# Attention with int8 feed-forward on one core: weights handed over transposed, split by scales from sums of squares or maxima, and values laid into key ranges through DRAM

## What is computed

```python
def _L0_attn_ref(x, wq, wk, wv, wo):
    ...
    q = (x @ wq.T).reshape(b, t, N_HEADS, HEAD_DIM).transpose(0, 2, 1, 3)
    k = (x @ wk.T).reshape(b, t, N_KV_HEADS, HEAD_DIM).transpose(0, 2, 1, 3)
    v = (x @ wv.T).reshape(b, t, N_KV_HEADS, HEAD_DIM).transpose(0, 2, 1, 3)
    ...
    scores = jnp.einsum('bhtd,bhsd->bhts', q, k_full) / np.sqrt(HEAD_DIM)
    mask = _sink_window_mask(t)[None, None, :, :]
    attn = _masked_softmax(scores.astype(jnp.float32), mask).astype(x.dtype)
    out = jnp.einsum('bhts,bhsd->bhtd', attn, v_full)
    out = out.transpose(0, 2, 1, 3).reshape(b, t, N_HEADS * HEAD_DIM)
    return out @ wo.T
...
x = x + _L0_attn_ref(_layernorm(x, axis=-1), L0_attn_wq, L0_attn_wk, L0_attn_wv, L0_attn_wo)
x = x + _L0_ffn_ref(_layernorm(x, axis=-1), L0_ffn_weight, L0_ffn_bias)
```

## Time and profile before

| what | value |
|---|---|
| median of 3 runs | 634.7 us (633.99 to 635.71) |
| profiled execution | 634.63 us, span 632.8 us |
| PE busy | 599.3 us (95%) |
| DVE busy | 544.8 us (86%) |
| ACT busy | 399.7 us (63%) |
| POOL busy | 307.8 us (49%) |
| mean granted clock of PE | 0.987 |

### The profile page before, as it was taken

How to read it: one execution, slowest core, us unless ns; L and a number is a source line. 1 busy time by engine, 2 the same in 40 slices (tenths; PEclk the granted TensorE clock), 3 DMA queues, 4 the chain that set the end, 5 groups by cost and what they waited for, 6 DMA issues and landing times.

```text
span 632.8 us, 18148 instructions
## 1 busy us (share of the span) xinstructions
PE 599.3 (95%) x7589; PEld 529.5 (84%) x7589; DVE 544.8 (86%) x1084; ACT 399.7 (63%) x631; POOL 307.8 (49%) x302
## 2 busy tenths in 40 slices
PE   5759999999999999999999999999999999999983
PEld 4547888889898988989898888989898888989872
DVE  5876899989898988989898998989898998988885
ACT  5676766566666666666666666667666666665740
POOL 1142445464565546455554646456554745535440
PEclk9989999999999999999999999999999999999996
DMA  9931401213040311203040221304030120304000
GB/s 295 352 103 20 116 1 49 55 35 85 3 117 2 86 34 46 73 15 105 1 120 2 67 52 37 83 9 112 3 96 24 53 68 20 99 1 118 3 18 34
DMA packets 33841, 41.31 MB, mean 65 GB/s; under 512 B 3936, under 2 KB 24416, under 8 KB 33760
## 3 DMA queue, kind: packets, MB, share of 16 engines
q1 hardware_dynamic: 33616, 40.02, 22.9%
q10 hardware_dynamic: 144, 0.13, 0.1%
HBM read 10.26 MB, written 4.19 MB: 23 GB/s over the span
## 4 chain that ended last, share of the span: by engine, by line
PE 87%; DVE 7%; ACT 3%; issue 1%; POOL 1%; DMA 1%; POOLq 0%; SPq 0%; ACTq 0%
PE ps L551 26%; PE ps L429 25%; PE ps L456 7%; PE ps L396 7%; PE ps L405 6%; PE ps L512 5%; PE ps L533 4%; PE ps L534 4%; PE ps L384 1%; PE ps L578 1%; DVE WoT L1008 1%; DVE Qs L892 1%; PE ps L566 1%; PE ps L336 1%; DMA X<-in_L_attn_x 1%
## 5 line engine op out<-in xcount | busy, mean ns | idle before, releaser
L429 PE MATMUL ps<-xT,WqT 128*128 128x256 f16 x1536 | 178.2, 273 | 2.0 <-DVE WqT L1008 1.3
L551 PE MATMUL ps<-WoT,pool 128*128 128x256 f16 x1536 | 178.0, 273 | 0.2 <-DVE pool L916 0.2
L429 PEld LDWEIGHTS ps<-xT,WqT 128*128 128x128 f16 x1536 | 147.0, 98 | 19.1 <-issue 3.0
L551 PEld LDWEIGHTS ps<-WoT,pool 128*128 128x128 f16 x1536 | 147.5, 98 | 16.4 <-DVE pool L916 0.3
L1203 POOL TENSOR_TENSOR small<-E,rr 128x576 f32<-128x576 f32 x63 | 72.6, 1152 | 99.8 <-DVE rr L911 99.8
L775 ACT ACTIVATE pool<-ps 128x512 f16<-128x512 f32 x128 | 69.5, 595 | 81.7 <-PE ps L534 81.6
L1209 POOL TENSOR_TENSOR PP<-small,PP 128x576 f16<-128x576 f32 x63 | 80.9, 1284 | 68.2 <-ACT PP L768 68.2
L735 ACT ACTIVATE Qs<-ps 128x576 f16<-128x576 f32 x128 | 82.4, 644 | 43.6 <-PE ps L429 43.6
L1195 POOL TENSOR_TENSOR Sm<-Sm,mx 128x576 f32<-128x576 f32 x64 | 73.7, 1152 | 54.2 <-DVE mx L902 52.9
L892 DVE TENSOR_TENSOR Qs<-ps,Qs 128x576 f16<-128x576 f32 x128 | 92.6, 724 | 3.2 <-ACT Qs L735 3.0
L916 DVE SCALAR_TENSOR_TENSOR pool<-ps,pool 128x512 f16<-128x512 f32 x128 | 81.8, 680 | 0.8 <-ACT pool L775 0.8
(11 more groups left out here) (110 smaller groups left out, 888.0 us busy)
## 6 DMA issues: line engine op xcount, KB each, us to landing
VW<-Vn SPq DMA_DIRECT2D x48, 120.0 KB
big<-Vn SPq DMA_DIRECT2D x48, 120.0 KB
X<-in_L_attn_x SPq DMA_DIRECT2D x16, 256.0 KB, 7.7
VW<-VW SPq DMA_DIRECT2D x16, 256.0 KB, 3.2
big<-big SPq DMA_DIRECT2D x16, 256.0 KB, 3.4
out<-pool SPq DMA_DIRECT2D x15, 256.0 KB, 3.6
big<-in_L_attn_wq SPq DMA_DIRECT2D x4, 512.0 KB, 7.6
pool<-in_L_attn_wo SPq DMA_DIRECT2D x4, 512.0 KB, 9.1
```

Source lines behind the costliest of these rows:

```text
L429: a = pe.matmul(banks[BANK_Q[f]][:, j * 256:j * 256 + 256], WqT[:, k, wl, h * 128:h * 128 + 128], xT[:, b % 2, k, xl, :], start=(n == 1), ...
L551: a = pe.matmul(banks[BANK_OUT][:, t * 256:t * 256 + 256], OT[:, p, ol, h, t * 128:t * 128 + 128], WoT[:, 4 * g + h, wl, :], start=first, ...
```

## The change

All four attention weights are handed over transposed, so that each tile arrives with the dimension over which PE sums in the partitions. The transposes on PE and their PSUM banks go, and so do `columns_up`, `maxima` and `maxima_out`.

- Scales: ACT squares a tile and sums it along the partitions (`weight_squares`, writing the squares into the place of the later high half) for k, q0, q1 and o0 to o3; for v, q2 and q3 DVE takes the largest magnitude (`weight_maximum`). PE adds the column over all partitions by one product with a matrix of 2^-10 (`scale_sums`; four products for o), DVE makes the power of two in three operations (`scale`). q1, q2 and q3 now have scales of their own.
- Halves: high halves on ACT from SBUF in one operation of 1024 for most tiles, those of v on POOL. Low halves on DVE for k, q0, q1 and o0; on POOL for v, q2, q3, o1, o2 and o3, where one operation multiplies the tile by its scale in place and a second subtracts the high half.
- The turned input of batch 0 is evacuated by DVE.
- New waits: ACT's `o_high` of units 0 and 1 waits for the low half of o0 and o1 (the attention output is written over those tiles), POOL's `p_norm` of these units for the low half of k and v, `pv` of unit 0 for the scale of o (it shares a bank with the sums), and `v_high` of a batch for the stores of the batch before instead of the copies.
- Values: each half of `Vn` is stored to a DRAM tensor `values`, and four loads of sinks and four of keys, each for four windows at once, bring them into the layout that `pv` reads; the upper partitions are loaded from DRAM too.
- Loads: the weights' transfers stand in another order (v before q0, q3 behind the output weights, the 64 KB identity `idf` late), and the inputs of batches 3 and later are loaded as the batches go.

The diff, cut to its core:

```diff
+                        sp.wait_ge(vw[i][p], 64 * (b // 2))
+                for t in range(2):
+                    sp.wait_ge(v_l, 2 * b + t + 1)
+                    sp.dma_start(kept[p, 128 * t:128 * t + 128], Vn[:, t, :, :]).then_inc(vd[p], 16)
                 if b > 1:
...
                 elif b == 1:
-                    sp.wait_ge(w_ps, w_at("q3", 1))
+                    for g in range(KV):
+                        sp.wait_ge(w_l[f"q{g}"], 2)
                     sp.dma_start(VW[1][64:128, :, 1, :], VW[0][64:128, :, 1, :]).then_inc(ld_z, 16)
...
+                sp.wait_ge(vd[p], 32 * (b // 2 + 1))
+                at_b = kept.offset + p * T * 1024
                 for i in range(2):
-                    sp.wait_ge(vw[i][p], 16 * (HALF_PIECES[i] + 1 - i) * (b // 2 + 1))
-                    sp.dma_start(VW[p][64:128, 4 * i:4 * i + 4, 0, :], VW[p][0:64, 4 * i:4 * i + 4, 0, :]).then_inc(vw2[i][p], 16)
+                    for ls, row in ((slice(0, 2), 0), (slice(0, 1), 64)):
+                        n = 512 * ls.stop
+                        sinks = bass.AP(kept.tensor, at_b, [[1024, 4], [0, 4], [1, n]])
+                        keys = bass.AP(kept.tensor, at_b + 4 * i * STEP * 1024, [[1024, KEYS - 4], [STEP * 1024, 4], [1, n]])
+                        to = VW[p][:, 4 * i:4 * i + 4, ls, :].rearrange("p w l n -> p w (l n)")
+                        sp.dma_start(to[row:row + 4], sinks).then_inc(vw[i][p], 16)
+                        sp.dma_start(to[row + 4:row + KEYS], keys).then_inc(vw[i][p], 16)
...
+            sp.dma_start(w_tile("q3"), wq_v[3]).then_inc(ld_q[3], 16)
+            load_x(2)
+            v_windows(0)
...
+            sp.dma_start(idf[:, :], idf_d).then_inc(ld_idf, 16)
+            load_x(3)
+            load_x(4)
             v_windows(1)
+            load_x(5)
             for b in range(2, B):
                 v_windows(b)
+                if b + 4 < B:
+                    load_x(b + 4)
...
+            def scale_sums(name):
+                tiles = [n for n in TILES if n[0] == "o"] if name == "o" else [name]
...
...
+                    pe.wait_ge(w_s[SUMS_ORDER[SUMS_ORDER.index(name) - 1]], 1)
+                for i, n in enumerate(tiles):
+                    pe.wait_ge(w_am[n], 1)
+                    a = pe.matmul(all_sums(name), small_ones[:, :], am[:, AM[n]:AM[n] + 1],
+                                  start=(i == 0), stop=(i == len(tiles) - 1))
+                a.then_inc(w_all[name], 1)
...
             pe.wait_ge(ld_idh, 16)
+            scale_sums("k")
             x_transpose(0)
-            columns_up("q0")
-            pe.wait_ge(ld_q[0], 16)
-            w_transpose("q0", big[:, 0, :], (0,))
-            maxima_out("q0")
-            w_transpose("q0", big[:, 0, :], (1,))
+            scale_sums("q0")
+            scale_sums("v")
             pe.wait_ge(xt_ok, 1)
             k_fill(0, 0)
             q_fill(0, 0)
-            columns_up("v")
             q_fill(0, 1)
-            maxima_out("v")
-            pe.wait_ge(ld_v, 16)
-            w_transpose("v", small[:, 1, :])
-            pe.wait_ge(ld_q[1], 16)
-            pe.wait_ge(w_l, l_at("k"))
-            w_transpose("q1", big[:, 1, :])
+            v_fill(0, 0)
             scores(0)
-            columns_up("q")
-            pe.wait_ge(w_l, l_at("v"))
-            v_fill(0, 0)
-            maxima_out("q")
+            scale_sums("q1")
             v_fill(0, 1)
             q_fill(1, 0)
             q_fill(1, 1)
-            pe.wait_ge(w_l, l_at("q1"))
-            pe.wait_ge(ld_q[2], 16)
-            w_transpose("q2", big[:, 2, :])
             kv_fill(0)
+            scale_sums("q2")
             x_transpose(1)
...
+            def weight_squares(name):
+                act.wait_ge(w_loaded(name), 16)
+                src, hi, _, _ = w_views(name, None)
+                act.activation(hi, src, ACT.Square, accum_out=am[:, AM[name]:AM[name] + 1]).then_inc(w_am[name], 1)
...
+                whole = len(js) == 2
+                act.wait_ge(w_s["o" if name[0] == "o" else name], SCALE_OPS)
+                if name in MAXIMA:
+                    act.wait_ge(w_loaded(name), 16)
+                src, hi, _, c = w_views(name, None if whole else js[0])
+                act.activation(hi, src, ACT.Copy, scale=up[:, c:c + 1]).then_inc(w_h[name], len(js))
...
+                if j == 0 and u < 2:
+                    act.wait_ge(w_l[f"o{u}"], 2)
...
+            weight_high("k", (0,))
+            weight_squares("q0")
+            weight_high("k", (1,))
+            weight_high("q0", (0,))
+            weight_high("q0", (1,))
             k_high(0, 0)
             q_high(0, 0)
             q_high(0, 1)
-            weight_sum(3, am[:, 2:3], big[:, 2, :], ld_q[2])
-            w_high("v")
-            weight_sum(4, am[:, 3:4], big[:, 3, :], ld_q[3])
+            weight_squares("q1")
             v_high(0, 0)
+            weight_high("q1")
             exps(0)
-            w_high("q1")
             v_high(0, 1)
+            weight_squares("o0")
+            q_high(1, 0)
+            q_high(1, 1)
             ln_split(1)
-            q_high(1, 0)
-            weight_sum(5, amo[:, 0:1], wo32[:, 0, :], ld_o[0])
-            q_high(1, 1)
-            w_high("q2")
+            weight_squares("o1")
+            weight_high("q2")
             k_high(0, 1)
             x_evac(1)
-            weight_sum(6, amo[:, 1:2], wo32[:, 1, :], ld_o[1])
-            weight_sum(7, amo[:, 2:3], wo32[:, 2, :], ld_o[2])
-            weight_sum(8, amo[:, 3:4], wo32[:, 3, :], ld_o[3])
+            weight_squares("o2")
+            weight_squares("o3")
...
                 if t == 2 or (g == 1 and t > 1 and b + 2 < B):
                     ln_split(b + 2)
-                if 1 <= t <= 4:
-                    w_high(f"o{t - 1}")
+                if 1 <= t <= 3:
+                    weight_high(f"o{t}")
...
+            def weight_low(name, js=(0, 1)):
+                whole = len(js) == 2
+                src, hi, lo, c = w_views(name, None if whole else js[0])
+                dve.wait_ge(w_h[name], js[-1] + 1)
+                dve.scalar_tensor_tensor(lo, src, up[:, c:c + 1], hi, ALU.mult, ALU.subtract).then_inc(w_l[name], len(js))
...
+            scale("k")
+            weight_maximum("v")
+            weight_low("k", (0,))
+            x_evac(0)
+            scale("q0")
+            scale("v")
+            weight_low("q0", (0,))
+            weight_low("q0", (1,))
+            exp_scale(0)
             k_low(0, 0)
             q_low(0, 0)
             q_low(0, 1)
-            scales("v")
-            w_low("v")
+            weight_low("k", (1,))
             s_max(0)
-            maxima("q")
-            scales("q")
-            exp_scales(1, KV, s_at("q"))
+            scale("q1")
+            v_low(0, 0)
+            weight_low("q1")
+            exp_scale(1)
+            v_low(0, 1)
             ln_stats(1)
-            w_low("q1")
-            v_low(0, 0)
+            probs(0)
             ln_norm(1)
-            v_low(0, 1)
-            probs(0)
+            weight_maximum("q2")
             q_low(1, 0)
             q_low(1, 1)
-            w_low("q2")
+            scale("q2")
+            exp_scale(2)
+            weight_maximum("q3")
             k_low(0, 1)
             ln_stats(2)
...
                 probs(t)
                 q_low(t + 1, 1)
                 if t == 1:
-                    maxima("o")
-                    w_low("q3")
-                    scales("o")
-                    dve.wait_ge(w_s, s_at("o"))
+                    scale("q3")
+                    exp_scale(3)
+                    scale("o")
+                    dve.wait_ge(w_s["v"], 2)
...
+            def weight_high(name):
+                src, hi, _, c = w_views(name, None)
+                pool.wait_ge(w_s[name], SCALE_OPS)
+                pool.tensor_scalar(hi, src, up[:, c:c + 1], None, ALU.mult).then_inc(w_h[name], 2)
+            def weight_low(name, js=(0, 1)):
+                src, hi, lo, c = w_views(name, None if len(js) == 2 else js[0])
+                pool.wait_ge(w_h[name], js[-1] + 1)
+                pool.tensor_scalar(src, src, up[:, c:c + 1], None, ALU.mult).then_inc(w_c[name], len(js))
+                pool.wait_ge(w_c[name], js[-1] + 1)
+                pool.tensor_tensor(lo, src, hi, ALU.subtract).then_inc(w_l[name], len(js))
...
                     pool.wait_ge(p_l, u - 1)
+                else:
+                    pool.wait_ge(w_l["kv"[u]], 2)
                 pool.tensor_tensor(Pn[:, p], E[:, p], rr[:, p, :].unsqueeze(2).to_broadcast([128, NT, KEYS]),
                                    ALU.mult).then_inc(p_n, 1)
...
             ln_low(0)
+            weight_high("v")
+            weight_low("v")
             s_shift(0)
             ln_rstd(1)
+            p_norm(0)
             ln_low(1)
-            p_norm(0)
+            weight_low("q2")
             ln_rstd(2)
             for t in range(1, NU - 2):
                 b, g = divmod(t, KV)
```

(7 more changed lines are left out.)

291 lines of the change are left out of this document (101 added, 190 removed).

## The result

The changed kernel takes 643.36 us, the median of 4 runs (640.94 to 647.06). The kernel before takes 635.21 us in the runs beside them. The ratio is 1.0135, with a 95% interval of 1.0106 to 1.0164. The forecast was 630.7 us, with a range of 628.2 to 633.6. So the sign was wrong, and the time lies 10 us above the upper end of the range.

The account below looks back on a forecast made before the run. PE was taken as the bound, with only the start of unit 6's scores able to move the time. Terms: 3.1 + 1.75 - 0.95 = 3.9 us gained, 634.6 - 3.9 = 630.7 us, range 628.2 to 633.6.

Parts of the forecast that it names:

- What bounds the kernel: Whole kernel: PE bounds it, and the change's whole effect is the time at which unit 6's scores start.
- Term 1: Units 2 to 4: output-weight transposes leave PE and query fills stop waiting for those weights, 3.1 us gained.
- Term 2: First two units: the new order brings scores 2 at 49.8 instead of 51.56, 1.75 us gained (0 to 3).
- the walk to scores 0: Opening, new order walked with old durations: scores 0 at 19.4 instead of 20.92 us.
- After 38: Sign of a wrong forecast: query fill 2 starting after 38 us; 36.8 to 37.9 was expected.
- The clock, nothing charged: PE's gaps before query fills 1 and 2: half rate there mostly fills gaps, so nothing further was charged.
- the clock stays up: Rival: 1.2 us more gained in the key fill before scores 2, 0.3 in unit 3; 629.2 us, chance 0.14.
- Term 3: POOL's weight work in units 1 to 4 delays the turning of input 2 in unit 3: 0.95 us lost.
- Values through DRAM: Value stores and loads through DRAM replace copies: costed at nothing, with 13 us of cover in the old path.
- The rival of late values: Values reach their products late: slower, needs 13 us of delay, each further one costs up to 16; chance 0.03.
- The wait for output weights 1 on ACT: ACT's attention output of unit 1 waits for POOL's low half: 0.6 us of cover, nothing charged.
- POOL holding up DVE: Rival: DVE's small operations and low halves wait beside POOL in the first units; 637.8 us, chance 0.09.

Follow-up runs that it names:

- E7: Changed kernel with LayerNorm's low half of batch 2 moved ahead on POOL and all work on the weights moved from POOL to ACT and DVE: 632.0 us.
- E11: E7 plus 8 throwaway matmuls on PE at the end of passes 2, 3 and 4, where weight transposes had stood: 634.25 us.
- E9: E7 plus throwaway matmuls in four of PE's waits, to keep PE busy: 627.89 us.
- E12: Changed kernel plus throwaway matmuls in six of PE's waits, POOL's work untouched: 640.12 us.
- E1: Changed kernel with values brought to their windows by the old SBUF copies, not through DRAM: 641.28 us.
- E8: Changed kernel with only the low halves of output weights 1 to 3 moved from POOL to DVE: 637.51 us.
- E4: Changed kernel with POOL's multiply of weights by their scale written with two tensor inputs instead of one: 637.76 us.
- E2: Changed kernel with LayerNorm's low half of batch 2 ahead of the first half of output weights 2 on POOL: 639.89 us.
- E10: E7 with values brought to their windows by the old SBUF copies, not through DRAM: 632.08 us.

## Why the prediction was wrong, point by point

**What bounds the kernel.** Right: nothing but the first units matters, and from there the same work stands as before. All fourteen profiles bear it out: the profiled time is the start of scores 9 plus 513.2 or 513.3 us plus 1.8, but for two with a half-rate stretch at the end. In terms of that sum, the forecast had scores 2 come 1.75 us sooner, and they came 5.4 later; it had another 2.15 us gained by scores 6, and 5.8 were lost between scores 2 and 4 alone. Both places failed alike. A small correction: an earlier start is not carried on quite whole. E7 leads before by 5.0 us at scores 6 (87.17 against 92.18) and by 4.3 at scores 9.

**Term 1, 3.1 us gained by PE.** Right in mechanism, and near enough in size, as E7 and E11 show it; in the changed kernel itself it lies under the waits for POOL. E7 gains 3.9 us between scores 2 and 6 (36.70 us against 40.62) and keeps 3.2 of it to scores 9. E11 gives back 2.25 for 2.8 us of throwaway matmuls, which stand for the 2.6 us of transposes alone. The waits of the query fills on the output weights went too, as was said.

**Term 2, 1.75 us gained in the first two units.** This is the step that failed first, at two places. One is the walk to scores 0: it had the value weights ready in time. The rule by which I bounded the one-input multiply, "between nothing saved, 2.3 us, and half of that, since it reads half as much", was an assumption with no row, and wrong in its direction: the three operations over the value weights took 3.23 + 2.84 + 2.27 us, 8.3 where 4.6 to 6.9 was allowed, and the value fill waited 4.2 us. Scores 0 came at 24.81, not 19.4. The price is not all of it: POOL began at 13.56, so that even at the walk's own prices, 5.7 us in all, the weights would have been ready near 19.3 (an estimate), over 1 us after the query fill ended at 18.1. The walk to scores 0 has no step for them. With the values off POOL they come at 19.3 to 20.4, so the rest of that walk was good. The other is query fill 2: it began at 45.02 and not by 37.9, 3.2 us of that for POOL. The other 4 us came down from the late scores 0. "After 38" was one of the signs of a wrong forecast, and it was met.

**The clock, nothing charged.** Wrong, and a cause of its own. "Half rate there mostly fills gaps" left out that a fill's end, not its start, sets what DVE and ACT do next. E9 shows 2.4 us of it by the profiles with POOL out of the way, and 4.1 by the medians; in the changed kernel it is some 2 to 4 us by the profiles (E12). The rival "the clock stays up" had this mechanism with 1.2 us; it needed a cause that keeps it up, and the change did the opposite. The key fill at half rate that I did keep in the sum was the smaller part.

**Term 3, 0.95 us lost.** Right place, wrong size. The wait of x's transposes on POOL in unit 3 was expected at about 1 us and was 4.2 (3.3 in E1). The term was worked out from the cost of one half of output weights 2 ahead of the step, 1.8 to 2.4 us; it measured 2.8 (1.56 + 1.19 and the gap between). But POOL also came to pass 3 late. Its shift began 5.4 us after scores 3, where the forecast had 2.5 and the kernel before 3.4. The halves of output weights 1 in pass 2 do that, and not their price: with them off POOL it is 3.5 us (E8), with the cheaper multiply 6.3 (E4). Between 60 and 85 us POOL was busy for 20.96 of 25 us, against 9.39 in the kernel before:

```profile
60.00:85.00 25.00, 20.18 (x206) 16.11 (x204) 13.86 (x24) 15.02 (x23) 20.96 (x17) 0.86 0.52 117
```

"Their POOL operations keep over 2 us of slack" looked at POOL's steps one by one, when at that load they form a queue, and one that also goes through ACT and DVE (E4). The "22 to 28 us" of POOL's work are a slip besides: the prices given there add up to 21.9 to 29.9, and 34.8 were measured. And 1158 against 738 ns, which the prediction took to bear out "about two times", is 1.6 times. The half clock behind the gap added 2.0 us (4.73 against 2.78) to the out-projection alone. E2 and E8 show both parts.

**Values through DRAM, nothing.** Right (E10). The rival of late values is out. The wait for output weights 1 on ACT does not show among PE's waits, as forecast.

**The rivals.** None of the four was it. The one that ended slower, POOL holding up DVE, is real but small here. DVE's two low halves of query weights 0, first in E7, where POOL is idle beside them, then in the changed kernel, beside the one-input multiply, then in E4, beside the two-input one:

```profile
12.99 1.41 DVE L952 SCALAR_TENSOR_TENSOR WqT<-big,up,WqT 128x512 f16<-128x512 f32 x2
```

```profile
13.32 2.27 DVE L951 SCALAR_TENSOR_TENSOR WqT<-big,up,WqT 128x512 f16<-128x512 f32 x2
```

```profile
12.45 3.05 DVE L951 SCALAR_TENSOR_TENSOR WqT<-big,up,WqT 128x512 f16<-128x512 f32 x2
```

That is 0.9 and 1.6 us of hold-up. At later places it is a microsecond now and then, and in unit 3 one such microsecond lay on the path to the wait (E4). No run takes it apart from POOL's own lateness, since what frees POOL frees DVE too. The true case was a fifth one that stood in the text as a bound to be covered: PE waits for POOL itself. The price of an operation without a row should have been let out upward too, and a slower rival worked out from it. By estimate, at 2.85 us for 1024 elements and not the 1.7 that I took, the two multiplies ahead of the value fill and the one ahead of query fill 2 are 3.5 us longer, and the forecast's 3.9 us are nearly gone before term 3 is touched.

## What to carry to other kernels

Work that is moved to a mostly idle engine is not free when it is put ahead of the few steps that others wait for: place each such step behind those, and add the moved work up over the stretch in which it falls, not over the span. Where an operation has no row in the trace, leave its price open on both sides, and see what a price well above the guess leaves of the gain (here it was two thirds above), before trusting the sum. And what is taken from TensorE in a stretch where it already waits may cost its clock: throwaway matmuls in the waits were worth 4.1 us here with POOL free, and with them, and nothing of the weights on GpSimd, the change is 1.0% faster than the kernel before (0.5% without them). Whether they would help the kernel before in its own 4.8 us wait was not tried.

## What the runs showed of the hardware

GpSimd's multiply by a per-partition scale, one tensor read, takes 1586 ns for 128x512 float32 and 2850 for 128x1024; the same product with the scale broadcast as a second tensor takes 1040 and 1892 to 2155. The Trainium skill, in GPSIMD Engine Reference, section 4.1, says that one-input work on GpSimd is near line rate. The form measured here does not fit that, and the measurement decides: it is 1.5 times as dear as the two-input form. VectorE does the whole low half, multiply and subtraction in one instruction, in 1285 ns for 1024 elements, where POOL needs 2850 + 2132.

The dearer form held up VectorE less, at the one place where the two can be compared: two instructions of VectorE took 2.27 us beside it (in five profiles alike) and 3.05 beside the two-input form (E4), against 1.41 alone.
